# One stream for attention's maxima, a chunk ahead, in a two-layer adaLN kernel

## What is computed

```python
c_kv = x @ W_kv_down
k_rope = _rotary_apply(c_kv @ W_k_rope, cos, sin)
k = (c_kv @ W_k_up).reshape(Bb, Tt, NH, HD)      # 16 heads of 16
v = (c_kv @ W_v_up).reshape(Bb, Tt, NH, HD)
scores = jnp.einsum('bqhd,bkhd->bhqk', q, k)
scores = scores + jnp.einsum('bqr,bkr->bqk', q_rope, k_rope)[:, None]
scores = scores / scale
scores = jnp.where(causal[None, None], -jnp.inf, scores)
w = jax.nn.softmax(scores, axis=-1)
attn = jnp.einsum('bhqk,bkhd->bqhd', w, v).reshape(Bb, Tt, D_MODEL)
```

## Time and profile before

| | |
|---|---|
| three runs | 1905.84 us median (1897.41 to 1908.26) |
| profiled execution, its own time | 1909.41 us |
| its span | 1907.5 us |
| PE, DVE, ACT busy | 1573.5, 1155.3, 881.4 us |
| mean granted TensorE clock | 0.92 |
| attention in the span | about 156 to 1120 us |

### The profile page before, as it was taken

How to read it: one execution, slowest core, us unless ns; L and a number is a source line. 1 busy time by engine, 2 the same in 40 slices (tenths; PEclk the granted TensorE clock), 3 DMA queues, 4 the chain that set the end, 5 groups by cost and what they waited for, 6 DMA issues and landing times. The chain is left out here.

```text
span 1907.5 us, 34704 instructions
## 1 busy us (share of the span) xinstructions
PE 1573.5 (82%) x13116; PEld 801.7 (42%) x13116; DVE 1155.3 (61%) x3193; ACT 881.4 (46%) x1252; POOL 341.1 (18%) x400
## 2 busy tenths in 40 slices
PE   7983689999999999999999958500999867889798
PEld 5440122333333333333333326300798734666476
DVE  3846779687887978778787008510566655212465
ACT  2330345666656666666666733400677624211132
POOL 2462880000000000000000012076111001100011
PEclk9995799999999999999999979655999968999899
DMA  8287440403014040220400026023767402882001
GB/s 287 105 258 174 133 135 14 82 15 76 20 40 69 27 82 14 64 33 32 77 27 27 15 102 227 22 97 96 90 87 90 54 7 70 278 293 73 12 33 56
DMA packets 102198, 166.60 MB, mean 87 GB/s; under 512 B 23596, under 2 KB 72492, under 8 KB 100884
## 3 DMA queue, kind: packets, MB, share of 16 engines
q1 hardware_dynamic: 83124, 113.15, 24.7%
q0 software_dynamic: 16112, 47.59, 7.9%
q10 hardware_dynamic: 2800, 3.64, 0.5%
HBM read 107.76 MB, written 56.47 MB: 86 GB/s over the span
## 5 line engine op out<-in xcount | busy, mean ns | idle before, releaser
L909 ACT ACTIVATE at_pr<-ps 128x1024 f32<-128x1024 f32 (+3 forms) x640 | 546.7, 894 | 347.6 <-PE ps L849 218.6
L942 DVE TENSOR_REDUCE at_mx<-ps 128x1 f32<-128x512 f32 x768 | 489.1, 685 | 144.9 <-PE ps L801 136.7
L939 DVE CUSTOM_DVE_ANT_0 at_seen<-ps,later 128x384 bf16<-128x384 f32 (+3 forms) x512 | 229.2, 486 | 15.9 <-issue 10.7
L849 PE MATMUL ps<-bq,bk 64*128 64x512 f16 (+3 forms) x1280 | 223.4, 346 | 0.0
L846 PE MATMUL ps<-sqk 64*128 64x512 f16 (+3 forms) x1280 | 172.2, 348 | 12.9 <-DMA sqk<-at_mr 12.9
L846 PE MATMUL ps<-at_sqk 64*128 64x512 f16 (+3 forms) x1280 | 170.7, 345 | 6.4 <-DMA at_sqk<-at_mr 5.6
L801 PE MATMUL ps<-sqk 64*128 64x512 f16 (+3 forms) x640 | 120.7, 374 | 60.1 <-DVE at_mx L942 29.5
L825 PE MATMUL ps<-at_pr,at_vl 128*32 128x512 f32 (+3 forms) x1280 | 150.0, 541 | 0.1
L825 PE MATMUL ps<-at_pr,vl 128*32 128x512 f32 (+3 forms) x1280 | 150.0, 541 | 0.0
L801 PE MATMUL ps<-at_sqk 64*128 64x512 f16 (+3 forms) x640 | 114.2, 354 | 20.6 <-DVE at_mx L942 8.3
L801 PEld LDWEIGHTS ps<-sqk 64*128 64x128 f16 x640 | 31.1, 94 | 208.0 <-DVE at_mx L942 123.7
(11 more groups left out here) (274 smaller groups left out, 2366.1 us busy)
## 6 DMA issues: line engine op xcount, KB each, us to landing
mi_tz<-d_z SPq DMA_DIRECT2D x32, 1024.0 KB, 7.2
ex_xr<-d_rows SPq DMA_DIRECT2D x39, 256.0 KB, 8.8
d_rows<-at_nil POOLq DMA_DIRECT2D x31, 322.0 KB
d_va<-st_va SPq DMA_DIRECT2D x8, 1024.0 KB, 4.3
d_o<-at_oc POOLq DMA_DIRECT2D x32, 256.0 KB, 2.3
at_pw<-in_w POOLq DMA_DIRECT2D x24, 256.0 KB, 3.3
d_w<-at_ph POOLq DMA_DIRECT2D x24, 256.0 KB, 2.4
exw<-d_w SPq DMA_DIRECT2D x8, 768.0 KB, 13.4
```

Of the source, the lines that this page charges most:

```text
L849: ins = pe.matmul(ps[:, 2 * f + r, off:CH], g.bk[half[r], b, k], g.bq[half[r], b, q], start=False, stop=t < 0)
L909: act.activation(pr[:, n % 2, f, :, off:CH], ps[:, 2 * f:2 * f + 2, off:CH], ACT.Exp, scale=INV_SCALE).then_inc(exp_done[f], 1)
L939: ins = dve.tensor_tensor_reduce(seen[:, turn, r, 0:n], src, g.later[:, CH - n:CH], 1.0, LOWEST, ALU.add, ALU.max, dst)
L942: ins = dve.tensor_reduce(dst, src, AX.X, ALU.max)
```

## The change

- Unit 0 takes its chunks in the order 2, 3, 1, 0 (`OPENING`). Before its first score stand the 24 pairs of chunk 2, a turn, and 6 pairs of chunk 3 (`BRIDGE`).
- Every chunk is turned by itself: 4 turns a unit instead of 2, each with its own 4 shift DMAs and its own semaphore.
- All pairs are one stream over the units. The pairs of the first chunk of the next unit and its turn end before step 37 of a unit, 4 pairs of its next chunk follow in steps 37 to 39 (`EARLY`), and the other pairs of a unit, with those of the next unit's first chunk, are spread over steps 0 to 36.
- `spread` puts each item at the first place whose estimated time is not before the summed estimate of VectorE's time up to it (`cost`, `places_of`), a turn 1000 ns later.
- In unit 0, 26 pairs lie in steps 0 to 11; then come a turn and 6 pairs at once, after step 11.
- A masked reduction waits for the reductions two diagonal pairs back, not for those just before it (`seen_at`).
- SyncE's queue has each unit's first shift, then the next unit's load, then the other three shifts.

Cut to its core; removed lines stand in the listing above:

```diff
-def attn_steps():
...
+def attn_steps(chunks):
+    return [(qc, kb) for qc in chunks for kb in range(TPC * (qc + 1))]
+def max_pairs(chunks):
+    return [(i, qc * TPC + t, j) for qc in chunks for t in range(TPC) for i in range(2) for j in range(qc + 1)]
 def phase_attention(nc, g):
-    STEPS, PAIRS = attn_steps(), max_pairs()
...
+    NU = NG * NB
+    OPENING, FALLING = [2, 3, 1, 0], [3, 2, 1, 0]
+    ORDER = [OPENING] + [FALLING] * (NU - 1)
+    STEPS = [attn_steps(o) for o in ORDER]
+    PAIRS = [max_pairs(o) for o in ORDER]
+    ENDS = [{qc: n for n, (qc, kb) in enumerate(st)} for st in STEPS]
+    NS, NPAIR = len(STEPS[0]), len(PAIRS[0])
     RING = 3
-    REST0 = 2 * N_PRE + 2
...
+    UNIT = 2 * NPAIR + NCH + 1
     INV_STEP = 24
-    def width(p):
-        _, qb, j = PAIRS[p]
+    def upto(v, m):
+        return sum(2 * TPC * (qc + 1) for qc in ORDER[v][:m])
+    def pair_slot(v, k):
+        return 2 * k + max(m for m in range(NCH) if upto(v, m) <= k)
+    def turn_slot(v, m):
+        return 2 * upto(v, m + 1) + m
+    def turned(v, m):
+        return v * UNIT + (turn_slot(v, m) + 1 if m + 1 < NCH else UNIT)
+    def width(v, k):
+        _, qb, j = PAIRS[v][k]
         return min(CH, (qb + 1) * P - j * CH)
-    DIAG = [p for p, (_, qb, j) in enumerate(PAIRS) if j == qb // TPC]
...
+    def diagonal(v, k):
+        _, qb, j = PAIRS[v][k]
+        return j == qb // TPC
+    def chunk_pairs(v, m, n0=0, n1=None):
+        k0, k1 = upto(v, m), upto(v, m + 1)
+        return [("pair", v, k) for k in range(k0 + n0, k1 if n1 is None else k0 + n1)]
+    def cost(x):
+        if x[0] == "turn":
+            return 1500
+        return 2 * (width(*x[1:]) + 150) + (120 if diagonal(*x[1:]) else 0)
+    def places_of(u, s0, s1):
+        now, out = 0, []
+        for s in range(s0, s1):
+            qc, kb = STEPS[u][s]
+            w = CH - max(kb - TPC * qc, 0) * P
+            score, product = 1.25 * w + 150, 1.7 * w + 130
+            out += [(now + score, (u, s, 0)), (now + 2 * score, (u, s, 1)), (now + 2 * score + product, (u, s, 2))]
+            now += 2 * score + product
+        return out, now
+    TODO = {(u, s, at): [] for u in range(NU) for s in range(NS) for at in range(3)}
+    def spread(items, whole, u, s0, s1):
+        spots, length = places_of(u, s0, s1)
+        rate = length / sum(cost(x) for x in whole)
         done = 0
-        for p, x in zip(range(n0, n1), cost):
...
+        for x in items:
+            at = (done + (1000 if x[0] == "turn" else 0)) * rate
+            TODO[next((p for t, p in spots if t >= at), spots[-1][1])].append(x)
+            done += cost(x)
+    BRIDGE, EARLY, LAST = 6, 4, 37
+    BEGIN = chunk_pairs(0, 0) + [("turn", 0, 0)] + chunk_pairs(0, 1, 0, BRIDGE)
+    first_end = ENDS[0][ORDER[0][0]] + 1
+    second = chunk_pairs(0, 1, BRIDGE)
+    spread(second, second, 0, 0, first_end)
+    TODO[0, first_end - 1, 2] += [("turn", 0, 1)] + chunk_pairs(0, 2, 0, BRIDGE)
+    for u in range(NU):
+        mine = []
+        for m in range(2 if u == 0 else 1, NCH):
+            mine += chunk_pairs(u, m, (BRIDGE if u == 0 else EARLY) if m == (2 if u == 0 else 1) else 0) + [("turn", u, m)]
+        v = min(u + 1, NU - 1)
+        ahead = chunk_pairs(v, 0) + [("turn", v, 0)]
+        spread(mine + ahead if u + 1 < NU else mine, mine + ahead, u, first_end if u == 0 else 0, LAST)
+        if u + 1 < NU:
+            early = chunk_pairs(v, 1, 0, EARLY)
+            spread(early, early, u, LAST, NS)
...
-            def shift(b, t0, t1, slots):
-                sp.wait_ge(mx_done, slots)
+            def shift(v, m):
+                b, qc = v % NB, ORDER[v][m]
+                sp.wait_ge(mx_done, turned(v, m))
                 for r in range(2):
                     for i in range(2):
-                        o = 8 * (2 * r + i) + (t0 - NT // 2 if t0 >= NT // 2 else 32 + t0)
...
+                        o = 32 * qc + TPC * (2 * r + i)
+                        sp.dma_start(g.sqk[b][64 * r + 63:64 * r + 64, 0, i, 1, qc * CH:(qc + 1) * CH]
+                                     .rearrange("p (t q) -> p t q", q=P), mr[o:o + TPC, b, :])\
+                          .then_inc(shift_ld[b][m], 16)
             fill_rope(sp, g, 1, once)
             load(0, 1)
-            MID = NT // 2
...
+            for m in range(NCH):
+                shift(0, m)
+            for u in range(1, NU):
+                shift(u, 0)
+                if u + 1 < NU:
+                    load(*divmod(u + 1, NB))
+                for m in range(1, NCH):
+                    shift(u, m)
...
+            def turn_maxima(v, m):
+                pe.wait_ge(mm_ready, NCH * v + m + 1)
+                pe.transpose(ps[:, MAXB + turn_slot(v, m) % RING, 0:P], mm[:, v % NB, :], g.ident[:, :]).then_inc(mt_ready, 1)
+            def ahead(items):
+                for kind, v, n in items:
+                    if kind == "turn":
+                        turn_maxima(v, n)
+                        continue
+                    if v and n == 0:
+                        if v == 1:
+                            pe.wait_ge(once, 16 * N_ROPE_LOADS)
+                        pe.wait_ge(ld[v % NB], loaded(*divmod(v, NB)))
+                    maxima(v, n)
+            ahead(BEGIN)
...
                 for s in range(NS):
-                    if first and s == chunk_end[3] + 1:
...
+                    if STEPS[u][s][1] == 0:
+                        pe.wait_ge(shift_ld[b][ORDER[u].index(STEPS[u][s][0])], 64 * (grp + 1))
                     scores(s, 0)
-                    for x in todo[:n0]:
-                        maxima(*x)
+                    ahead(TODO[u, s, 0])
                     scores(s, 1)
-                    for x in todo[n0:n0 + n1]:
...
+                    ahead(TODO[u, s, 1])
+                    if s == 0 and u:
                         weighted(*before, NS - 1)
                     if s >= 1:
                         weighted(grp, b, s - 1)
-                    for x in todo[n0 + n1:]:
...
+                    ahead(TODO[u, s, 2])
...
+            seen_at = []
+            def pair(v, k):
+                i, qb, j = PAIRS[v][k]
+                n, slot = width(v, k), pair_slot(v, k)
+                dve.wait_ge(mx_ready, v * NPAIR + k + 1)
+                turn = len(seen_at) % 2
+                if diagonal(v, k):
+                    if len(seen_at) >= 2:
+                        dve.wait_ge(mx_done, seen_at[-2])
+                        dve.memset(gap[:, :], 0.0)
+                    seen_at.append(v * UNIT + slot + 2)
...
+            def turn_maxima(v, m):
+                b, qc, slot = v % NB, ORDER[v][m], turn_slot(v, m)
+                dve.wait_ge(mx_done, v * UNIT + slot)
+                dve.tensor_reduce(mm[:, b, 32 * qc:32 * qc + HG * TPC].rearrange("p (h t) -> p h t", h=HG),
+                                  mx[:, :, qc * TPC:(qc + 1) * TPC, 0:qc + 1], AX.X, ALU.max).then_inc(mm_ready, 1)
+                rows = slice(32 * qc, 32 * qc + HG * TPC)
+                dve.wait_ge(mt_ready, NCH * v + m + 1)
                 dve.tensor_scalar(mr[rows, b, :], ps[rows, MAXB + slot % RING, 0:P], -1.0 / SHIFT_UNIT, None, ALU.mult)\
-                   .then_inc(mx_done, slots)
...
+                   .then_inc(mx_done, turned(v, m) - (v * UNIT + slot))
+            def ahead(items):
+                for kind, v, n in items:
+                    if kind == "turn":
+                        turn_maxima(v, n)
+                    else:
+                        pair(v, n)
+            ahead(BEGIN)
...
```

More of the change, by code:

```diff
@@ L668, in phase_attention @@
         ld = [sem(f"ld{b}") for b in range(NB)]
-        shift_ld = [sem(f"shift_ld{b}") for b in range(NB)]
+        shift_ld = [[sem(f"shift_ld{b}_{m}") for m in range(NCH)] for b in range(NB)]
         mx_ready, mx_done = sem("mx_ready"), sem("mx_done")
@@ L729, in body @@
                 u = index(grp, b)
-                for i, qc in enumerate(qcs):
+                for i, qc in enumerate(ORDER[u]):
                     pool.wait_ge(out_moved, u * NCH + i + 2)
@@ L790, in _, with maxima @@
-            shift(1, 0, MID, NG * NB * UNIT)
+            for m in range(NCH):
[6 more added lines that the diff above has]
+                    shift(u, m)
         @block.tensor
         def _(pe):
[L794 to L799, removed]
+            def maxima(v, k):
+                i, qb, j = PAIRS[v][k]
+                b, slot = v % NB, pair_slot(v, k)
+                lo, hi_ = j * CH, j * CH + width(v, k)
+                if v * UNIT + slot > 1:
+                    pe.wait_ge(mx_done, v * UNIT + slot - 1)
@@ L803, in maxima @@
                 ins.then_inc(mx_ready, 1)
[L805 to L812, removed]
+            def turn_maxima(v, m):
[12 more added lines that the diff above has]
+            ahead(BEGIN)
             def weighted(grp, b, n):
                 u = index(grp, b)
-                qc, kb = STEPS[n]
+                qc, kb = STEPS[u][n]
```

(39 more changed lines are left out.)

99 lines of the change are left out of this document (7 added, 92 removed).

## The result

Nine runs of the changed kernel have a median of 1890.69 us (1881.83 to 1894.74), nine of the kernel before 1912.71 (1897.41 to 1917.31): the ratio is 0.9892, 95% interval 0.987 to 0.9915. Forecast were 1874 on the first median of 1905.84, a ratio of 0.983, so faster as forecast, by about two thirds of the amount. The time lies outside the forecast's own 1866 to 1882 and inside the stated range. The profiled execution's span went from 1907.5 to 1886.6.

The account below looks back on a forecast made before the run. TensorE and VectorE run in lockstep, neither full; evenness of pairs counts. Opening -10.3, unit 0 -19.1, units 1 to 6 -8.8, unit 7 +6.4 sum to -31.8, giving 1874 us on the median of 1905.8; range 1850 to 1901.

Parts of the forecast that it names:

- the opening: Before the first score: 8 fewer full-width pairs at 1.40 save 11.2, the score waits 0.9 longer; gain 10.3 us.
- Unit 0: First score to unit 1's first score: fewer pairs at 0.28 each, 121.4 us instead of 140.5, so 19.1 less.
- rival B: Middle units: the even stream brings nothing, they stay at 112.5; 1882 to 1890 us; chance 0.32 together with rival D.
- Rival D: Bridge pairs after step 11 and in the opening add to the DMA; +7 in all, 1886 us; chance 0.32 with rival B.
- The lump: Unit 0 after step 11: six pairs at once fit inside chunk 3's shift, turn included, priced at 6.0 us.
- Units 1 to 6: Middle units: four terms sum to -1.3 us each, so 111.2 a unit; with one extra gain -8.8 in all.
- The turns: Middle units: four turns instead of two, now amid pairs, at 0.5 each: 2.0 against 0.3, cost 1.7 us.
- The masked reduction: Middle units: the loosened wait cuts VectorE's idle time at masked reductions; gain 0.8 us a unit, bounds 0 and 2.
- Evenness: Middle units: pairs spread more evenly over the full-width steps; gain 1.0 us a unit, bounds 0.2 and 1.8.
- Unit 7: Last unit: 44 pairs instead of 24 and three turns for one; +6.4 us, to 100.7, bounds 98 and 106.
- Rival A: Middle units: placing pairs by VectorE's time removes most lockstep stalls, 107 us a unit, 1849 in all; chance 0.14.
- The clock: Unit 0's chunk 3 would start at 1.2 GHz despite the bridge: zero difference, at most 1.5 us more, outside the sum.

Follow-up runs that it names:

- old plan: The changed kernel with the previous kernel's step plan in units 1 to 7, each chunk still turned by itself; a middle unit took 116.0 us, unit 0 142.3.
- old places: The changed kernel with pairs of turnless steps in units 1 to 7 put into the previous kernel's places, same pairs per step; a middle unit took 111.0 us.
- two a step: The changed kernel, from unit 0's step 12 on with two pairs per step in second and third place, few exceptions; a middle unit took 108.4 us.

## Why the prediction was right, and the terms that failed

The direction was right because of the opening and unit 0, which brought 28.1 of the 29.4 forecast for them. In the middle units, where the forecast had its own mechanism, rival B came true: they stayed at 112.5 to 112.9, and the ratio of 0.989 on the first median of 1905.84 gives 1885, inside B's 1882 to 1890. That the time lies in the stated range is owed to B standing in it. (Rival D's 1886 stands 12 above the forecast, though its text says +7 in all; the run without bridges speaks against D at either price.)

- **The opening** was right: -10.0 for -10.3, with the bridge pairs and not the DMA ending last, and without the first unit's new order attention was 8.7 longer. Two small misses offset: the 8 pairs brought 11.7 (48.4 to the 36.7 without bridges) where 11.2 was priced, and the bridge delayed the score by 1.8, not 0.9.
- **Unit 0** was right to 1.0. The price of 0.28 a pair is an average and held only as one: the runs without bridges and with the old plan showed 0.55 to 0.9 in denser steps. The lump was priced at 6.0 and took 7.3 (8.9 against 1.6 for an equal step without pairs), since its six pairs end after the DMA. That unit 0 came out close despite this is luck in part, since the clock, taken as 2, is mixed in it.
- **Units 1 to 6** failed by 9.8 (+1.0 for -8.8), of the 12.8 that the forecast missed in attention. A unit came out at +0.34 for -1.3. Of its four terms the DMA wait at the unit's end was right: step 39 went from 2.83 to 1.60, and unit 6's extra 1.0 went with it. The turns were 0.3 too cheap, 4 x 0.56 = 2.3 instead of 2.0.
- **The masked reduction** is the largest miss: priced at -0.8 a unit (4.8 over six), worth 0. "Issue" as releaser was read as the wait that the change loosens. Undoing the loosening changed nothing, and the idle time had grown under it. It is most likely time without a pair to reduce: with the plain reductions halved it grew to 101.0.
- **"Evenness"** was priced at -1.0. What is left of the measured change, 0.34 + 1.2 - 2.0, is -0.5: inside its bounds, half its size (3.2 over six units). This rest also holds whatever two more reductions of the table cost and any error in the 0.3 for the old turns. The count of pairs by step was right, the price of a two-pair step was not: 2.8 came from the earlier trace rows, where the two stand in the second and third place, as the old rule always puts two. The placing by VectorE's summed time puts them in any places, and such steps then mostly take 3.1 to 3.5 (step 5 of unit 2, in the first and third place: 3.1, and 2.8 with the old places). With the old places the same counts gain 1.9 more, so the evenness alone is worth 2.4, above its bound of 1.8, and the new placing takes 1.9 of it back. The prediction had this in rival B ("neighbouring places are 0.6 to 0.9 of TensorE's work apart") and gave it a chance of its own instead of applying it to the two-pair steps.
- **Unit 7** was right in kind, 1.7 too small, for the same reason: its 44 pairs stand in the same placing, and with the old places it took 100.3, 2.0 less, and with two a step 96.6, 5.7 less.
- **Rival A** was left at 0.14 because a step has only three places. Its 107 was not reached by the change, but a plan with the same three places reaches 108.4: the limit was the plan, not their number.
- **The clock**: it fell under the bridge, as it had fallen in the idle wait before, and chunk 3 ran at the lower level for its first 3.0 us, as chunk 2 had for 3.3 before. This is the zero difference that the prediction drew from the rule of the Trainium skill, "TensorE: Matmul & The Clock Gate", Part 1; its further 1.5 did not come.

What stays open: why a wait at the first place costs more than the same wait elsewhere was not taken apart. The traces show the late pair holding back the second score and with it ScalarE's second exponential, but no run separates this from VectorE's own delay. Nor does any run show why the clock fell behind the turn of step 6 in units 2 to 7 of the old plan and not in unit 1.

## What to carry to other kernels

Where one engine feeds another through a ring one item deep, the total of work per stretch says little: look at how much of the producer's other work lies between two neighbours, at every pair of places, the one across the loop's edge too. Price a step by rows that have the same items in the same places, not only the same number. A round trip between two engines was cheap here (0.56) where its wait was filled by work already queued, and three times dearer (1.5 to 1.7) where it stood right behind what it waits for, six times (3.2) where the clock fell as well.

## What was not expected of the hardware

Behind a wait of 1.66 us of TensorE in the middle of an otherwise full unit, the granted clock stood at 0.53 over the next 3 us; this nearly doubled the price of the wait, from 1.7 to 3.2, and the same wait in unit 1 was not followed by a fall. And the phases that no edit touches varied by 33 us from trace to trace (931.5 to 964.5), while attention repeats within 1: 941.4 and 940.6 for the same kernel in two jobs.
